# First attention and banded attention each in one written-out order, the neighbour sequences' projection, rotation and output between the heads; x loaded by sequence

## The chip, the cores and the metric

One NeuronCore of a Trainium2 chip runs one program. The metric is its device time in microseconds. Engines: TensorE (PE; its weight loads are PEld in the profile), VectorE (DVE), ScalarE (ACT), GpSimd (POOL) and SyncE (SP), which here only issues DMAs.

## The reference

Two layers of a decoder over x (4 sequences x 512 tokens x 512) in float32. Layer 0: an attention of 16 heads of 32 with 4 key/value heads and rotary positions, a residual and a layernorm; a mixing step with a context and experts of low rank; layer 1: an attention limited to a band, with biases, an RMS norm of queries and keys and rotary positions; a cross attention; rounds with a workspace. The two attentions are what the change touches:

```
q, k, v = x W_q, x W_k, x W_v           # layer 1: + biases; q, k normalised by their RMS per head
q, k = rope(q), rope(k)
p = softmax(q k^T * scale)              # layer 1: only keys j with 0 <= i - j <= 64
x = layernorm(x + (p v) W_o)            # layer 1: + bias
```

## The kernel before

The program is five stages, one function each, one after another: `rope_attention` (line 353, "stage 1"), `mixing_and_experts`, `window_attention` (line 1138, "the banded stage"), `cross_attention`, `workspace_rounds`. Every engine has an instruction order of its own, written out by Python loops; semaphores join them. PSUM has eight banks; `Banks` counts who filled and who freed each. `Core.start` (line 248) loads x, one DMA per sequence, and the identity, and ends in a wait for all five, before any stage begins.

Both attentions are staged alike and share the function `turns`, which gives the order of the parts on every engine:

```
heads(b); project(b + 1); output(b); keys(b + 1)      # b = 0, 1, 2; before them project(0), keys(0)
heads(3); output(3)
```

- **project**: PE transposes the 512 tokens of x in four blocks (line 598, stage 1; line 293, banded), ACT rounds each to float32r (line 302), DVE keeps the rest (line 309). Then for each tile t of 128 tokens, 24 products by three (lines 198 to 200, `split3`) of the halves of x and of W_q|W_k|W_v: 512 columns of queries into one bank, 256 of keys and values into the next. In stage 1 DVE reads them from PSUM: the cosine product (line 721), two sine products (line 732), and their sum (line 552). ACT copies values and four parts of the rotated queries and keys (lines 491 to 498), POOL subtracts the rounded parts (lines 462, 463) to fill the stacks `qs`, `ks`. In the banded stage DVE first adds biases (1379), takes mean squares (1384), ACT their square root (1303), DVE normalises (1394) and does the sine products (732), POOL the cosine product (721) and the stacks (1269, 1270), DVE the sum (1402).
- **keys**: PE transposes four key stacks (616; 1472), ACT copies them (508; 1330).
- **heads** of stage 1: a list `steps` of twenty rounds i, each of four steps t. In round i PE forms the four score tiles s of head i (634), whose maxima DVE takes (573), transposes the maxima of head i-1 (m, 642), forms the four transposed score tiles e of head i-2 (648), to which ACT applies the exponential (530), and transposes the queries of head i+1 (q, 627). Heads go in groups g of four. In rounds 4g+6 and 4g+7 PE multiplies the group's probabilities by values (o, 663) and by ones (666); POOL adds three of a head's four probability tiles first (472, 474) into `x_cur`, which has room for one group, so that from head 4 on its sums wait until the group before is full. In rounds 4g+8 and 4g+9 DVE divides (quotients d: 559, 561), and only then PE may start the next group. s has two banks, e three, q and m one, o two.
- **heads** of the banded stage: twenty-one rounds; per head one transpose of queries (1483) that DVE copies (1424), one block of scores with the mask (1490, 1494), one exponential (1340); every four rounds the attention products (1505, 1513) and quotients (1432, 1434).
- **output**: PE multiplies by W_o, four tiles (676; 1525); DVE adds x and takes statistics (327, 329, 338, 340), POOL raises to the power -0.5 (349), DVE normalises (344).

The weights are split by ACT (484; 1292) and POOL (454; 1254) before PE begins. The banded stage loads x anew into `x_cur` (284) and POOL adds the output bias to x (1261).

Of the kernel before, what the change touches and what calls it, by code (L numbers as in the profile page):

```python
# [202 lines left out]
class Core:  # L203


    def __init__(self, nc, ctx, d):
# [32 lines left out]
        self.s1_stacked, self.s4_stacked = primed("s1_stacked", T), primed("s4_stacked", T)  # L239
        self.s4_v_out, self.s4_roped = primed("s4_v_out", T), primed("s4_rope_parts", T)  # L240
# [4 lines left out]
        self.consts = sem("consts_loaded")  # L245
        self.pool_consts = sem("pool_consts_set")

    def start(self, stage):

        block = stage.enter_context(self.nc.Block())  # L250

        @block.sync
        def _(sp):
            for b in range(B):
                sp.dma_start(self.x[:, b * T:(b + 1) * T, :], self.d["x"][b].rearrange("(t p) d -> p t d", p=P)) \
                  .then_inc(self.consts, 16)
# [96 lines left out]
def rope_attention(c):  # L353

    nc, d, ps = c.nc, c.d, c.ps
    with ExitStack() as ctx:
        def sb(nm, shape, dt=F32):
            return ctx.enter_context(nc.sbuf_tensor(f"s1_{nm}", shape, dt))

        wq_hi = sb("wqkv_hi", [P, KD, NQKV], F32R)  # L360
        wq_lo = sb("wqkv_lo", [P, KD, NQKV], F32R)
        wo = sb("wo", [P, KD, D])
        qs = sb("q_stacks", [P, T, NH, STK])
# [5 lines left out]
        v = sb("v", [P, T, NK])  # L369
        v_next = sb("v_next", [P, T, NK])  # L370
        NPB = 6
        probsT = sb("probsT", [P, NPB, T, S])
        outT = sb("outT", [P, 4, S])
        inv = sb("inv_sums", [P, S])
        ra = sb("rope_a", [P, 2, NQK * HD])
        rb = sb("rope_b", [P, NQK * HD])
        cs = sb("cos_sin", [P, T, 2, HD])
        wraw = probsT[:, 0:3, :, :].rearrange("p a b c -> p (a b c)")[:, 0:KD * NQKV] \
            .rearrange("p (k n) -> p k n", k=KD)

        weights = c.sem("s1_weights_loaded")
        w_hi = c.sem("s1_w_hi_ready")
        w_lo = c.sem("s1_w_lo_ready")
        frame = c.sem("s1_constant_rows_set")
        roped = Count(c.sem("s1_roped"), T)
        v_out = Count(c.sem("s1_v_out"), 1)
        r_hi = Count(c.sem("s1_rope_hi"), T)
        stacked = c.s1_stacked
        added = Count(c.sem("s1_probs_added"), NH)

        steps = [("q", 0)]
        for i in range(NH + 4):
            g, r = (i - 6) // 4, (i - 6) % 4
            for t in range(T):
                if i < NH:  # L400
                    steps.append(("s", i, t))
                if 0 <= i - 2 < NH:
                    steps.append(("e", i - 2, t))
                if t == 0 and 0 <= i - 1 < NH:
                    steps.append(("m", i - 1))
                if t == 2 and i + 1 < NH:
                    steps.append(("q", i + 1))
                if 0 <= g < 4 and r < 2 and t % 2 == 0:
                    steps.append(("o", g, 2 * r + t // 2, 0))
                if 0 <= g < 4 and r == 1 and t % 2:  # L410
                    steps.append(("o", g, t // 2, 1))
                if 0 <= g < 4 and r >= 2 and t % 2:
                    steps.append(("d", g, 2 * (r - 2) + t // 2))

        steps = [s for s in steps if s[:2] != ("d", NKV - 1)]
        uses = []
        n = {"s": 0, "e": 0}
        for s in steps:
            if s[0] in "qm":
                uses.append((s, 5, 1))  # L420
            elif s[0] == "s":
                uses.append((s, n["s"] % 2, 1))
                n["s"] += 1
            elif s[0] == "e":
                uses.append((s, 2 + n["e"] % 3, 1))
                n["e"] += 1
            elif s[0] == "o" and s[2:] == (0, 0):
                uses.append((("o", s[1]), 6, 2))


        ps.open_segments({
            "heads": uses,
            "project": c.x_uses([2, 3]) + [(("p", t), (0, 3)[t % 2], 2) for t in range(T)],
            "output": c.y_uses([2, 5]),
            "keys": [(("k", g), (0, 1)[g % 2], 1) for g in range(NKV)]})

        block = ctx.enter_context(nc.Block())

        @block.sync
        def _(sp):  # L440
            sp.dma_start(wraw, d["l0a_wqkv"].rearrange("(k p) n -> p k n", p=P)).then_inc(weights, 16)
            sp.dma_start(cs[:, :, :, :], d["cos_sin"].rearrange("(t p) a n -> p t a n", p=P)).then_inc(weights, 16)
            sp.dma_start(wo[:, :, :], d["l0a_wo"].rearrange("(k p) n -> p k n", p=P)).then_inc(weights, 16)

        @block.gpsimd
        def _(pool):
# [4 lines left out]
            pool.memset(nmax[:, :, :, :], 0.0).then_inc(frame, 1)  # L451

            pool.wait_ge(w_hi, 1)
            pool.tensor_tensor(wq_lo[:, :, :], wraw, wq_hi[:, :, :].bitcast(F32), ALU.subtract).then_inc(w_lo, 1)

# [2112 lines left out]
```

## Time and profile before

| | us |
|---|---|
| median of 3 runs | 2774.46 (2773.37 to 2779.09) |
| the profiled execution | 2771.16, its span 2769.4 |
| PE busy | 2235.7 (81%) |
| DVE busy | 1512.0 (55%) |
| ACT busy | 1152.3 (42%) |
| POOL busy | 922.0 (33%) |

Times in the profile count from the span's start. PE's busy time has modelled ends of matmuls and is no measure of how well it is used. A line's "idle before, releaser" says what ended the engine's wait. A mean granted clock of 1.00 is TensorE's full clock.

### The profile page before, as it was taken

Reading aid. Unit: us, or ns where it says so; the run is one execution under the profiler, and the core shown is the slowest. Engines: PE = TensorE matmul, PEld = TensorE weight load, DVE = VectorE, ACT = ScalarE, POOL = GpSimd, SP = SyncE. Lnnn points to the kernel's source line nnn. Section 1 sums busy time; section 2 is a strip of 40 time slices with the busy share of each in tenths; the row PEclk is TensorE's granted clock in tenths of the full one; section 3 lists DMA queues with packets and bytes.
Section 4 is the critical chain, followed back from the end, with each engine's and each line's share of the span. In section 5 each row is a group of like instructions: output and inputs, shape, how many; then the busy total and the mean of one; then the engine's idle time right before and its main releaser. Section 6 shows DMA issues by size and latency. Waiting matters only on the chain. (4 is left out here: it accounts for less than half of the span.)

```text
span 2769.4 us, 34033 instructions
## 1 busy us (share of the span) xinstructions
PE 2235.7 (81%) x11600; PEld 1532.0 (55%) x11624; DVE 1512.0 (55%) x2234; ACT 1152.3 (42%) x2123; POOL 922.0 (33%) x553
## 2 busy tenths in 40 slices
PE   3888888857893668667699999999999999967672
PEld 3444545436672445444477777777777777743340
DVE  1656565634554475664255575557555755543435
ACT  2636363623422332322355555555555555531322
POOL 2424243420003120220355555555555555530101
PEclk9999999978996889888899999999999999988796
DMA  2000000010002000000311121112111111120001
GB/s 102 1 1 1 1 1 1 1 52 6 1 1 84 1 16 16 1 1 1 108 46 45 45 69 45 45 45 68 45 45 45 46 46 45 45 98 0 0 1 61
DMA packets 63213, 88.84 MB, mean 32 GB/s; under 512 B 6224, under 2 KB 41424, under 8 KB 62096
## 3 DMA queue, kind: packets, MB, share of 16 engines
q1 hardware_dynamic: 63120, 87.60, 9.4%
q8 instruction: 59, 0.97, 0.1%
q14 instruction: 34, 0.28, 0.0%
HBM read 75.00 MB, written 4.19 MB: 29 GB/s over the span
## 5 line engine op out<-in xcount | busy, mean ns | idle before, releaser
L1826 DVE RECIPROCAL s_inv_sums<-banks 128x512 f32<-128x512 f32 x64 | 214.8, 3356 | 343.2 <-PE banks L1939 339.8
L1700 POOL TENSOR_TENSOR s_qk_rstd<-s_mean_sq,minus_half 128x8 f32<-128x8 f32 x64 | 118.5, 1852 | 501.2 <-DVE s_mean_sq L1813 501.2
L573 DVE TENSOR_REDUCE s_neg_max<-banks 128x1 f32<-128x512 f32 x256 | 169.9, 687 | 117.6 <-PE banks L634 117.3
L1932 PE MATMUL banks<-s_probsT,s_v 128*128 128x512 f32 x512 | 230.8, 593 | 0.0
L1763 ACT ACTIVATE s_probsT<-banks,s_minus_bound,s_qk_rstd 128x512 f32<-128x512 f32 x256 | 177.0, 782 | 92.4 <-PE banks L200 88.4
L530 ACT ACTIVATE s_probsT<-banks 128x512 f32<-128x512 f32 x256 | 145.2, 599 | 107.8 <-PE banks L648 106.9
L198 PE MATMUL banks<-s_w_proj_hi,xT_hi 128*128 (+1 forms) x512 | 170.2, 332 | 2.9 <-DVE s_ctxT_lo L1874 2.9
L1932 PEld LDWEIGHTS banks<-s_probsT,s_v 128*128 128x128 f32 x512 | 97.5, 190 | 110.9 <-issue 108.2
L1734 ACT ACTIVATE s_squares<-banks 128x512 f32<-128x512 f32 x64 | 38.2, 597 | 286.6 <-PE banks L200 286.6
L1693 POOL TENSOR_TENSOR s_w_proj_lo<-s_w_proj_raw,s_w_proj_hi 128x2048 f32 (+1 forms) x33 | 152.0, 4607 | 12.7 <-ACT s_w_proj_hi L1726 12.7
L634 PE MATMUL banks<-s_kT,s_qT 96*128 96x512 f32 x256 | 123.1, 486 | 40.6 <-DVE s_neg_max L573 24.7
L1709 POOL TENSOR_TENSOR s_probs_pair_sums<-s_probsT 128x1024 f32<-128x1024 f32 x64 | 151.1, 2361 | 7.2 <-issue 7.2
L472 POOL TENSOR_TENSOR x_cur<-s_probsT 128x512 f32<-128x512 f32 x64 | 81.5, 1274 | 201.1 <-PE banks L666 139.4
L199 PE MATMUL banks<-s_w_proj_lo,xT_hi 128*128 (+1 forms) x512 | 145.3, 284 | 0.0
L200 PE MATMUL banks<-s_w_proj_hi,xT_lo 128*128 (+1 forms) x512 | 145.3, 284 | 0.0
L721 POOL TENSOR_TENSOR s_rope_a<-s_proj,s_cos_sin_gain 128x512 f32<-128x512 f32 (+1 forms) x32 | 29.9, 955 | 274.4 <-DVE s_proj L1394 274.4
L634 PEld LDWEIGHTS banks<-s_kT,s_qT 96*128 96x128 f32 x256 | 49.7, 195 | 125.2 <-issue 62.0
L1340 ACT ACTIVATE s_probsT<-banks,s_minus_bound 128x896 f32<-128x896 f32 x64 | 64.5, 1008 | 119.6 <-PE banks L1494 119.6
L198 PE MATMUL banks<-s_w_out_hi,s_outT_hi 128*128 (+1 forms) x256 | 104.2, 407 | 5.8 <-DVE s_outT_lo L1833 5.8
L198 PEld LDWEIGHTS banks<-s_w_proj_hi,xT_hi 128*128 128x128 f32 x512 | 98.4, 192 | 18.1 <-issue 18.1
L198 PE MATMUL banks<-s_w_proj_hi,s_ctxT_hi 128*128 (+1 forms) x256 | 101.5, 396 | 7.1 <-ACT s_v L1749 7.1
L199 PEld LDWEIGHTS banks<-s_w_proj_lo,xT_hi 128*128 128x128 f32 x512 | 98.5, 192 | 14.8 <-issue 14.8
(382 smaller groups left out, 6079.0 us busy)
## 6 DMA issues: line engine op xcount, KB each, us to landing
s_w_proj_raw<-l1x_wq SPq DMA_DIRECT2D x33, 512.0 KB, 4.7
s_w_out_raw<-l1x_wo SPq DMA_DIRECT2D x33, 512.0 KB, 3.9
s_w_proj_raw<-l1x_wk SPq DMA_DIRECT2D x33, 256.0 KB, 5.0
s_w_proj_raw<-l1x_wv SPq DMA_DIRECT2D x33, 256.0 KB, 5.1
x_cur<-x_all SPq DMA_DIRECT2D x8, 1024.0 KB, 6.9
x_all<-x SPq DMA_DIRECT2D x4, 1024.0 KB, 9.2
s_ctxT<-ctxT SPq DMA_DIRECT2D x8, 512.0 KB, 5.1
out<-x_all SPq DMA_DIRECT2D x4, 1024.0 KB, 4.3
```

What stands on the lines that cost most here:

```text
L198: pe.matmul(out, lhs[0], rhs[0], start=start, stop=False)
L199: pe.matmul(out, lhs[0], rhs[1], start=False, stop=False)
L200: return pe.matmul(out, lhs[1], rhs[0], start=False, stop=stop)
L530: act.activation(probsT[:, h % NPB, k, :], ps.ap(s), ACT.Exp).then_inc(ps.freed(s), 1)
L573: dve.tensor_reduce(nmax[:, h % 2, t, 0:1], ps.ap(s), AX.X, ALU.max, negate=True) \
L634: pe.matmul(ps.ap(s), qT[0:STK, h % NQB, t * P:(t + 1) * P], kT[0:STK, h % NKV, :], start=True, stop=True).then_inc(ps.filled(s), 1)
L1693: pool.tensor_tensor(out, raw, hi.bitcast(F32), ALU.subtract).then_inc(done.sem, 1)
L1700: pool.tensor_tensor(rs[:, j, :, :], ms[:, j, :, :], c.mhalf[:, 0:T * HP].rearrange("p (t h) -> p t h", h=HP), ALU.pow) \
L1709: pool.tensor_tensor(psum2[:, :, :], probsT[:, h, 0:2, :], probsT[:, h, 2:4, :], ALU.add)
L1763: act.activation(probsT[:, h, k, :], pb.ap(("e", h, k)), ACT.Exp, bias=bound[:, 0:1], scale=rs[:, 1, k, h:h + 1]).then_inc(pb.freed(("e", ...
L1826: dve.reciprocal(inv[:, h, :], pb.ap(("sum", h))).then_inc(pb.freed(("sum", h)), 1)
L1932: mm = pe.matmul(pb.ap(("o", h)), v[:, k, h * DX:(h + 1) * DX], probsT[:, h, k, :], start=(k == 0), stop=(k == T - 1))
```

## The change

Both functions drop `turns` and their parts. One list `seq` of steps (phase, sequence, ...) is built, and every engine walks the whole of it and does what of a step is its own. New phases: X (transpose of a block of x), Pq and Pk (a tile's query product; its key and value product), R (sine on DVE, cosine on POOL; in the banded stage normalisation before and the sum after), A (the sum, stage 1), H (ACT's copies and POOL's stacks), Y (a tile of the output product with its addition), L (normalisation), S (square roots of four tiles). In round i, step t, of sequence b in stage 1:

```
            extra = {(i, t): [] for i in range(LAST) for t in range(T)}
            if b > 0:
                for t in range(T):
                    extra[0, t].append(("d", b - 1, NKV - 1, t))
                    extra[t + 1, 1].append(("Y", b - 1, t))
                extra[5, 3].append(("L", b - 1))
            if b + 1 < B:
                for k in range(KD):
                    extra[4 + k // 2, 1 + k % 2 * 2].append(("X", b + 1, k))
                for t in range(T):
                    i = 7 + 2 * t if t < NPJ else 15
                    extra[i, 1].append(("Pq", b + 1, t))
                    extra[i + 1, 0].append(("Pk", b + 1, t))
                    extra[i + 1, 1].append(("R", b + 1, t))
                    extra[i + 1, 2].append(("A", b + 1, t))
                    extra[14 + t, 3].append(("H", b + 1, t))
```

and in the banded stage:

```
            if b > 0:
                for t in range(T):
                    extra[t].append(("Y", b - 1, t))
                extra[5].append(("L", b - 1))
            if b + 1 < B:
                for k in range(KD):
                    extra[2 + k].append(("X", b + 1, k))
                extra[14].append(("S", b + 1))
                for t in range(T):
                    extra[6 + 2 * t].append(("Pq", b + 1, t))
                    extra[7 + 2 * t].append(("Pk", b + 1, t))
                    extra[14 + t].append(("R", b + 1, t))
                    extra[15 + t].append(("H", b + 1, t))
```

The core of the rest, stage 1:

```diff
-            sp.dma_start(self.ident[:, :], self.d["ident"]).then_inc(self.consts, 16)
-            sp.wait_ge(self.consts, 16 * (B + 1))
...
+            sp.dma_start(c.ident[:, :], d["ident"]).then_inc(first, 16)
+            load_x(0, first)
+            sp.dma_start(w, d["l0a_wqkv"].rearrange("(k p) n -> p k n", p=P)).then_inc(weights, 16)
...
-            pool.tensor_tensor(wq_lo[:, :, :], wraw, wq_hi[:, :, :].bitcast(F32), ALU.subtract).then_inc(w_lo, 1)
+            pool.tensor_tensor(w_l[:, 0:2, :], w[:, 0:2, :], w_h[:, 0:2, :].bitcast(F32), ALU.subtract).then_inc(w_lo_pool, 1)
...
+                if ph == "R":
+                    t = s[0]
+                    pool.wait_ge(*sin_done.after(b, t + 1))
+                    rope_cos(pool, pj[:, t % NPJ, :], pj[:, t % NPJ, :], cs, t).then_inc(cos_done.sem, 1)
...
+                elif ph == "Pq":
+                    t = s[0]
+                    act.wait_ge(*ps.full(0, ("Pq", b, t)))
+                    if t >= NPJ:
+                        act.wait_ge(*stacked.after(b, t + 1 - NPJ))
+                    act.activation(pj[:, t % NPJ, 0:D], ps.ap(("Pq", b, t)), ACT.Copy).then_inc(ps.freed(("Pq", b, t)), 1)
...
+                elif ph == "L":
+                    act.wait_ge(*nmr_ready.after(b, 1))
+                    for t in range(T):
+                        xt = c.x[:, b * T + t, :]
+                        act.activation(xt, xt, ACT.Identity, bias=nmr[:, t:t + 1], scale=c.rstd[:, t:t + 1])
...
+                elif ph == "R":
+                    t = s[0]
+                    dve.wait_ge(*projected.after(b, t + 1))
+                    dve.drain()
+                    rope_sin(dve, pj[:, t % NPJ, :], rb, cs, t).then_inc(sin_done.sem, 1)
+                elif ph == "A":
+                    t = s[0]
+                    dve.wait_ge(*sin_done.after(b, t + 1))
+                    dve.wait_ge(*cos_done.after(b, t + 1))
+                    dve.tensor_tensor(pj[:, t % NPJ, :], pj[:, t % NPJ, :], rb[:, :], ALU.add).then_inc(roped.sem, 1)
```

NPJ is 3: the projected queries and keys go by ACT copies into three buffers in SBUF, where sine and cosine read them. DVE's step `d` of group 3 falls in round 0 of the next sequence. X, Pq, Pk and Y of the rounds use bank 4, which was the third bank of e; e keeps two. Values have two buffers instead of a copy. In the banded stage the same pieces use bank 3 (queries keep bank 2 alone); biases come into the products as one more product with a row of ones (four DMAs of single rows instead of two broadcast over 128 partitions); ACT instead of DVE reads the projection and copies queries; x is not loaded anew and POOL's addition to it goes; ACT waits for the weights alone before it splits them, POOL and DVE each take half of the low part; S takes the four tiles' roots at once.

## Rows read from the trace of the kernel before

**Rows 1.** Busy time by stretch (us, PE, PEld, DVE, ACT, POOL, PEclk, DMA, GB/s)
```profile
202.00:294.70 92.70, 79.72 (x444) 38.06 (x443) 57.31 (x92) 52.19 (x95) 40.41 (x32) 0.96 0.00 1
...
970.00:987.00 17.00, 16.99 (x97) 15.01 (x98) 14.10 (x24) 5.05 (x12) 1.89 (x2) 1.00 0.16 63
...
1081.00:1197.00 116.00, 81.02 (x579) 53.96 (x585) 72.45 (x109) 33.91 (x55) 20.08 (x18) 0.85 0.03 10
```

**Rows 2.** PE's timeline at the seams of stage 1 (start us, us, engine, line)
```profile
66.55 1.73 PE L616 MATMUL banks<-ident_sb,s_k_stacks 128*96 128x128 f32 x7 [6.23 <-POOL s_k_stacks L463]
...
294.73 1.09 PE L598 MATMUL banks<-ident_sb,x_all 128*128 128x128 f32 x8
...
316.61 13.90 PE L676 MATMUL banks<-s_wo,s_outT 128*128 128x512 f32 x32
330.35 1.04 PE L616 MATMUL banks<-ident_sb,s_k_stacks 128*96 128x128 f32 x8
```

**Rows 3.** PE's timeline, transposes of the maxima in five rounds
```profile
210.38 0.60 PE L642 MATMUL banks<-ident_sb,s_neg_max 128*32 128x128 f32 x4
...
214.07 0.60 PE L642 MATMUL banks<-ident_sb,s_neg_max 128*32 128x128 f32 x4
...
253.19 0.60 PE L642 MATMUL banks<-ident_sb,s_neg_max 128*32 128x128 f32 x4 [0.18 <-DVE s_neg_max L573]
...
260.72 0.60 PE L642 MATMUL banks<-ident_sb,s_neg_max 128*32 128x128 f32 x4
...
264.85 0.60 PE L642 MATMUL banks<-ident_sb,s_neg_max 128*32 128x128 f32 x4
```

**Rows 4.** Timeline of the end of a turn, POOL and PE
```profile
282.55 1.28 POOL L472 TENSOR_TENSOR x_cur<-s_probsT 128x512 f32<-128x512 f32 x1 [11.53 <-PE banks L666]
...
287.75 4.48 PE L663 MATMUL banks<-s_probsT,s_v 128*32 128x512 f32 x24 [1.06 <-DVE s_outT L561]
...
293.73 1.07 PE L666 MATMUL banks<-x_cur,ones_sb 128*32 128x512 f32 x8
```

**Rows 5.** Timeline of the start, ACT and POOL
```profile
25.46 2.76 ACT L484 ACTIVATE s_wqkv_hi<-s_probsT 128x3072 fp32r<-128x3072 f32 x1 [8.84 <-DMA s_wo<-l0a_wo]
28.30 6.65 POOL L454 TENSOR_TENSOR s_wqkv_lo<-s_probsT,s_wqkv_hi 128x3072 fp32r<-128x3072 f32 x1 [8.81 <-ACT s_wqkv_hi L484]
```

**Rows 6.** Groups of instructions by form, 0 to 600 us (busy, mean ns | idle)
```profile
L573 DVE TENSOR_REDUCE s_neg_max<-banks 128x1 f32<-128x512 f32 x256 | 169.9, 687 | 117.6 <-PE banks L634 117.3
...
L474 POOL TENSOR_TENSOR x_cur<-x_cur,s_probsT 128x512 f32<-128x512 f32 x64 | 81.7, 1276 | 9.1
...
L559 DVE RECIPROCAL s_inv_sums<-banks 128x128 f32<-128x128 f32 x64 | 60.7, 948 | 9.8 <-PE banks L666 9.7
...
L462 POOL TENSOR_TENSOR s_q_stacks<-s_rope_a,s_q_stacks 128x512 fp32r<-128x512 f32 x16 | 20.6, 1289 | 93.0 <-ACT s_k_stacks L498 93.0
L561 DVE TENSOR_TENSOR s_outT<-banks,s_inv_sums 128x128 f32<-128x128 f32 x64 | 18.7, 292 | 5.1 <-issue 0.4
...
L552 DVE TENSOR_TENSOR s_rope_a<-s_rope_a,s_rope_b 128x640 f32<-128x640 f32 x16 | 14.3, 892 | 1.2
L732 DVE TENSOR_TENSOR s_rope_b<-banks,s_cos_sin 128x320 f32<-128x320 f32 x32 | 14.1, 481 | 0.0
...
L495 ACT ACTIVATE s_q_stacks<-s_rope_a 128x512 fp32r<-128x512 f32 x16 | 10.0, 623 | 0.0
```

**Rows 7.** Timeline of one rotation of the banded stage, POOL and DVE
```profile
886.89 1.86 POOL L721 TENSOR_TENSOR s_rope_a<-s_proj,s_cos_sin_gain 128x512 f32<-128x512 f32 x2 [4.67 <-DVE s_proj L1394]
886.90 1.53 DVE L732 TENSOR_TENSOR s_mask_f<-s_proj,s_cos_sin_gain 128x256 f32<-128x256 f32 x1
```

**Rows 8.** Timeline of the banded stage: first product, first keys, last quotient's start
```profile
867.67 0.77 PE L198 MATMUL banks<-s_wqkv_hi,xT_hi 128*128 128x512 f32 x1 [1.61 <-DVE xT_lo L309]
...
910.16 3.71 PE L1472 MATMUL banks<-ident_sb,s_k_stacks 128*96 128x128 f32 x16 [23.62 <-POOL s_k_stacks L1270]
...
1306.36 0.96 DVE L1432 RECIPROCAL s_wqkv<-banks 128x128 f32<-128x128 f32 x1 [6.45 <-PE banks L1513]
```

More of the change, by code:

```diff
@@ L415, in rope_attention, with cnt @@
-        steps = [s for s in steps if s[:2] != ("d", NKV - 1)]
+        nmr = sb("ln_minus_mean_rstd", [P, T])
+        w = probsT[:, 0:3, :, :].rearrange("p a b c -> p (a b c)")[:, 0:KD * NQKV].rearrange("p (k n) -> p k n", k=KD)
+        def cnt(name, per=1):
+            return Count(c.sem("s1_" + name), per)
+        first, weights, table = c.sem("s1_first_x_loaded"), c.sem("s1_weights_loaded"), c.sem("s1_table_loaded")
+        wo_in = c.sem("s1_wo_loaded")
+        x_in = [None] + [c.sem(f"s1_x{b}_loaded") for b in range(1, B)]
@@ L671, in output, with turned @@
-            def output(b, pos):
-                pe.wait_ge(*ps.released(at("heads", pos[0]), ("o", NKV - 1)))
-                for t in range(T):
-                    ps.wait_empty(pe, pos, ("y", t))
+            pe.wait_ge(first, 32)
+            def turned(key, rows, source):
+                ps.wait_empty(pe, 0, key)
+                for t in range(T):
+                    mm = pe.transpose(ps.ap(key)[0:rows, t * P:(t + 1) * P], source(t), c.ident[:, :])
+                mm.then_inc(ps.filled(key), 1)
@@ L1287, in _, with turned_hi @@
-            turns(pool, project, nothing, nothing, output)
+                elif ph == "L":
+                    pool.wait_ge(*var_ready.after(b, 1))
+                    pool.tensor_tensor(c.rstd[:, :], c.veps[:, :], c.mhalf[:, 0:T], ALU.pow).then_inc(rstd_ready.sem, 1)
         @block.scalar
         def _(act):
-            act.wait_ge(weights, 16 * 9)
-            act.activation(w_h[:, :, :], w[:, :, :], ACT.Copy).then_inc(w_hi, 1)
+            def turned_hi(b, k):
+                act.wait_ge(*ps.full(0, ("X", b, k)))
+                act.activation(c.xhi[:, k, :], ps.ap(("X", b, k)), ACT.Copy).then_inc(x_hi.sem, 1)
@@ L1531, in window_attention, with projected @@
-        c.close(B)
+                    mm = pe.transpose(ps.ap(key)[0:rows, t * P:(t + 1) * P], source(t), c.ident[:, :])
+                mm.then_inc(ps.filled(key), 1)
+            def projected(key, b, t, lo, hi):
+                out = ps.ap(key)[:, 0:hi - lo]
+                ps.wait_empty(pe, 0, key)
+                for k in range(KD):
+                    split3(pe, out, (c.xhi[:, k, t * P:(t + 1) * P], c.xlo[:, k, t * P:(t + 1) * P]),
+                           (w_h[:, k, lo:hi], w_l[:, k, lo:hi]), k == 0, False)
+                if b == 0 and t == 0:
+                    pe.wait_ge(bias_lo, 1)
+                pe.matmul(out, ones[:, :], bias[:, lo:hi], start=False, stop=True).then_inc(ps.filled(key), 1)
```

1033 lines of the change are left out of this document (545 added, 488 removed).

## The prediction

> **What bounds the kernel now.** I read the busy table by stretch, then TensorE's (PE's) timeline at the seams between a sequence's parts, then one step of every round, then what GpSimd (POOL) and VectorE (DVE) wait for. Stage 1 runs from 0 to 588 us, the banded stage from 837 to 1333. While the sixteen heads of stage 1 run, no engine is full: PE 79.7 of 92.7 us, DVE 57.3, ACT 52.2, POOL 40.4; in a banded turn of 116.0 us PE has 81.0, DVE 72.5, POOL 20.1 [rows 1]. In stage 1 a turn is followed by a serial part: X and projection from 294.7 to 316.6 (21.9 us), output product to 330.35 (13.7 us), then keys [rows 2]. A round of the head loop, measured from one transpose of the maxima to the next, takes 3.7 us plain, 7.5 us with six attention products in it or before it, and 4.1 us where DVE has its first two quotients [rows 3]. So before the change the path is PE's order, with short waits for DVE; only at the end of a turn do POOL and DVE set it: POOL begins the sums of a group of heads at 282.55, having idled 11.5 us for the group before; PE's next attention product waits for DVE's quotients until 287.75, and its last, which needs POOL's sums, starts at 293.73 [rows 4].
>
> The profiled execution took 2771.2 us (span 2769.4 and 1.8 around it), the median shown is 2774.5, 3.3 above it. The sum goes against 2771.2.
>
> **Stage 1, start.** The four loads of x and their barrier go; weights are asked for at about 2 us and not about 15 (25.46 less the 8.84 of wait and the start of ACT's block). ACT had waited for weights, table and output weights, split at 25.46, POOL's low half took 6.65 us from 28.30, and only then PE could start, at 35 [rows 5]. After: about 2.6 MB must land first; from the old weight wait (as many bytes, some 10 us after issue) I take 11.5 us, ACT done at 14.3, POOL's half of the subtraction 3.3 us with DVE's beside it, projection starts near 17.6. But for sequence 0 the steps of a tile are now serial in ACT's order: copies 0.9, DVE's two sine products 0.7, POOL's cosine 1.6 (640 of width against 1.28 for 512), sum 0.9, four ACT copies 1.5 [rows 6], with hand-offs 6.1 us a tile, while PE needs 4.2 (17.0/4 [rows 1]). First projection done at 24; three more tiles 18.5, the first chain and POOL's end 7: keys at 49.4 instead of 66.5 [rows 2]. **-17**, and +2 because PE idles some 14 us before them: **-15**.
>
> **Stage 1, rotations between heads (three turns).** X and projection now lie in the rounds. PE's pieces are a query product of 2.75 us and a key product of 1.4 (17.0/4 in 2:1 of width [rows 1]). The crux is POOL's queue. Its sums for heads 4 and 5 stand ahead of R(0), and wait for group 0 of the attention, full only as round 7 ends; heads 8 and 9 ahead of R(2), heads 12 and 13, and H(0), H(1), ahead of R(3). Each sum is 2 x 1.28 plus a drain, 2.65 us [rows 6]. DVE waits in A for the cosine, and behind A stands its next maximum, without which PE can't transpose maxima. From the end of round 7: POOL sums to 5.6; DVE's sine reads SBUF and ends at 6.2; cosine to 7.9; A; maximum 0.7; transpose. What else each round gets is PE's piece or DVE's:
> - rounds 4, 5 (four X): +2.4; round 7 (query product): +2.8
> - round 8: 10.1 instead of 4.1, its key product inside that: +6.0; round 12 the same: +6.0
> - round 9: +1.2; round 10 (POOL free, but sine, cosine and sum in series on DVE): +3.0; round 11: +2.8; rounds 13 and 14: +0.5; round 15: +2.8
> - rounds 16 to 19: ACT's copy of tile 3 waits for H(0), which stands behind head 12's sums: ACT free at 4.7 after group 2 is full, POOL's row is then 12, H0, 13, H1, cosine 3 (end about 12.6), A to 14.5, three quotients of 1.24 (0.95 and 0.29 [rows 6]) to 18.3, then the last 24 products, 7 us: 25.4 against 12.3 (282.4 to 294.7): +13.1. POOL's stacks end at 23, inside that.
> Sum 40.6 for the 21.9 removed [rows 2]: +18.7 a turn, **+56**.
>
> **Two SBUF inputs.** In the banded stage a sine product of 256 columns took 1.53 us where POOL's cosine started 0.01 us before it [rows 7], and one of 320 columns took 0.48 in stage 1, where it reads PSUM [rows 6]. The change makes stage 1 read SBUF too, with POOL adding probabilities meanwhile. So I let A wait for one POOL add (1.1 us) in round 8, round 12 and the tail: 3.3 of the 40.6. Without it the whole sum is 10 us lower. The Trainium skill, "SBUF — State Buffer", section "Who interferes with whom", says that a DVE instruction with two SBUF inputs and a GpSimd instruction reading SBUF exclude each other for the whole instruction; by that rule the 3.3 stands, without it it would go; the trace agrees with the rule in those two rows.
>
> **Stage 1, output between heads (three turns).** Round 0 gets four quotients in front of maxima: +2.1; round 1 the first output block, waiting for them: +3.1; rounds 2 to 4 get 3.45 us each of PE less the 0.6 us that the plain round idles: +8.6. L: DVE waits at (5,3) for POOL's power, behind head 3's sums, then four ACT normalisations (2.4) stand before exponentials: +4.2, and +1.5 in two turns where X(3) follows. 18.0 for 13.7: **+13**, and **+3**. The end of the stage: one hand-off more, **+1**. Two score banks instead of three: 0; ACT's exponential had finished two products earlier in the plain rounds, and where ACT is held up PE is held by DVE too (if not, 1 us a round, in 9 rounds of three turns, +27).
>
> Stage 1: -15 + 56 + 13 + 3 + 1 = **+58**.
>
> **Banded stage.** Start: ACT splits when the weights land, not the last table, halves on two engines, X hidden: projection 17.5 us before 867.67; but the rotations of sequence 0 now all follow it: chain R0 4.4 + 3 x 6.6 + 3.8 = 28, where 23.6 us of waiting stood. Keys 8 us before 910.16 [rows 8]: **-8**. Each tile's 6.6 is POOL's cosine 1.9, sum 0.8, ACT's copies 1.8, POOL's stacks 1.75 and hand-offs: POOL does H(t-1) before the cosine of t [rows 6, 7]. Turns: PE's 81.0 [rows 1] less 8.5 for rounds 14 to 20 (estimate: two score blocks, one group and a quarter), plus 9 for keys, queries, X and output in one bank each, gives R(0) at 81 us; then the same chain of 28: 109 instead of 116. Rounds 14 to 20 hold only 12 us of other work, so that chain is bare. Without Y (turn 0) 92; without projection (turn 3) to the last group 70. 92 + 109 + 109 + 70 = 380 for 396.2 (910.16 to 1306.36 [rows 8]): -16, of which +3 for a PE that idles some 15 us in each tail (clock, below), the last normalisation +1: **-12**. The biases put into the products cost 1.4 and 0.9 us of PE a turn, inside the 109; what leaves DVE and POOL for it (bias additions) wasn't on the path after the keys. Queries and normalisation that ACT takes over from DVE cost nothing: ACT has 33.9 of 116 us [rows 1]; under that cover gone they would add 0.6 us a head. New bias loads stand on SP behind the weights and land before ACT has split those.
>
> In the banded turns PE's granted clock averaged 0.85 [rows 1], between its two levels (1.2 and 2.4 GHz), after waits in the rotations; longer ones come.
>
> Total +58 - 8 - 12 = **+38**: 2809 for the profiled execution, and 3.3 more for the median: **2812 us**.
>
> **Rivals.** (A, the forecast, 0.50.)
> (B, faster, 0.22) POOL doesn't decide: if sums of heads 4, 5, 8, 9, 12, 13 run before DVE needs the cosine (if ACT and PE lag enough behind, that is if R begins over 5.6 us after the group is full), rounds 8 and 12 cost 1.8 each and the tail 3. A turn falls by 20.4, three by 61: 2812 - 61 = 2751. For it: 13 us of PE idle in every head loop [rows 1]. Against: the 11.5 us wait of POOL for PE before its sums [rows 4] is in the order itself and stays.
> (C, slower still, 0.15) the two score banks bind: 2812 + 27 = 2839.
> (D, nearly level, 0.13) only the tails bind, rounds 8, 10 and 12 hide under PE's pieces: 4.2 + 4.2 + 2 a turn less, 2812 - 31 = 2781.
> That the change doesn't do what it says is excluded: the order is written out.
>
> **Numbers.** A measurement of this kernel tells 0.2% (5.5 us) from nothing. Faster: B and a few of A and D, 0.27; same: part of D, 0.06; slower 0.67. The range takes D, A, most of C and half of B: 2750 to 2842; A's own is 2790 to 2830.
>
> **What would show it.** Right: keys of sequence 0 near 49 us; turns of stage 1 near 155 us from key step to key step instead of 132; DVE's sum waiting for POOL's cosine about 2 us in rounds 8 and 12, 5 or more in round 16; ACT held at tile 3; in the banded stage about 28 us from the first rotation to the keys, PE mostly idle. Wrong: a stage 1 turn under 132 us, POOL's cosine never waited for, or PE busy over 90% of stage 1.

## The result and the profile after

The changed kernel took **2867.5 us** (median of 4 runs, 2866.5 to 2867.8); the kernel before, run beside it, 2776.8. The ratio is 1.0326, 95% interval 1.0311 to 1.0342. The direction was as forecast, the size was not: +91 us where +38 was forecast, and outside the range. The profiled execution has a span of 2864.6 us against 2769.4: 95.2 more, which is what the traces can be asked about.

Busy time of the changed kernel by stretch (stretch, its length, then PE, PEld, DVE, ACT, POOL with instruction counts, PEclk, DMA, GB/s). The first is the loop over heads of sequence 1, for 202.00:294.70 of [rows 1]; the second is a whole turn, keys to keys:

```profile
202.00:346.20 144.20, 111.22 (x518) 60.58 (x518) 73.66 (x117) 58.62 (x110) 41.57 (x33) 0.87 0.00 1
198.20:365.60 167.40, 127.65 (x612) 68.31 (x608) 79.92 (x126) 70.03 (x136) 55.12 (x45) 0.86 0.00 1
```

The same turn of the kernel before, in the same view:

```profile
198.10:330.30 132.20, 115.42 (x609) 62.90 (x608) 80.95 (x133) 64.59 (x125) 48.25 (x41) 0.97 0.00 1
```

And of run eleven below, which has its pieces between the heads as well:

```profile
176.80:307.90 131.10, 116.19 (x608) 63.97 (x608) 76.94 (x127) 69.92 (x136) 54.88 (x45) 0.93 0.00 1
```

A turn issues the same TensorE work in all three. Before, it filled 115.4 of 132.2 us, so at that clock 17 us a turn were all that any order could win. The change did not win them: in the turn shown TensorE idles 40 us, and its products take 12 us longer, at a granted clock of 0.86 for 0.97.

TensorE's timeline of the changed kernel (start, duration, engine, line, in brackets the idle time before and what ended it). The four key steps answer to 66.55 and 330.35 of [rows 2]; then transposes of the maxima, which mark the rounds as in [rows 3]: a round lasts from its transpose to the next. First those of rounds 8, 9 and 10 of turn 0, then of rounds 1 to 5 of turn 3:

```profile
53.85 3.71 PE L658 MATMUL banks<-ident_sb,s_k_stacks 128*96 128x128 f32 x16 [14.38 <-POOL s_k_stacks L500]
...
102.36 0.60 PE L658 MATMUL banks<-ident_sb,s_neg_max 128*32 128x128 f32 x4
112.55 1.01 PE L658 MATMUL banks<-ident_sb,s_neg_max 128*32 128x128 f32 x4 [2.95 <-issue]
120.53 0.60 PE L658 MATMUL banks<-ident_sb,s_neg_max 128*32 128x128 f32 x4
...
198.25 0.97 PE L658 MATMUL banks<-ident_sb,s_k_stacks 128*96 128x128 f32 x7
...
365.61 0.64 PE L658 MATMUL banks<-ident_sb,s_k_stacks 128*96 128x128 f32 x4
...
532.88 1.08 PE L658 MATMUL banks<-ident_sb,s_k_stacks 128*96 128x128 f32 x8
...
544.32 1.01 PE L658 MATMUL banks<-ident_sb,s_neg_max 128*32 128x128 f32 x4 [1.01 <-DVE s_neg_max L621]
554.35 0.60 PE L658 MATMUL banks<-ident_sb,s_neg_max 128*32 128x128 f32 x4
561.65 0.60 PE L658 MATMUL banks<-ident_sb,s_neg_max 128*32 128x128 f32 x4
568.94 0.60 PE L658 MATMUL banks<-ident_sb,s_neg_max 128*32 128x128 f32 x4
577.20 0.71 PE L658 MATMUL banks<-ident_sb,s_neg_max 128*32 128x128 f32 x4
```

The turns, key step to key step: 144.4, 167.4, 167.3, and 125.7 from the last keys to the last quotient (658.53). Before: 131.6, 132.2, 133.4 and 97.6. That is 109.9 longer in all, against keys of sequence 0 that stand 12.7 earlier. The last instruction before the banded stage ends 98.3 us later than before (935.5 for 837.2), and between it and the rotary stage nothing was changed. A plain round takes 3.6 us as before, a round with an output tile 7.3, the first of them 10.0. Rounds 7 and 8 take 10.3 and 10.2 us; bare, that is without any of the moved work, they take 7.5 and 4.1.

The banded stage of the changed kernel (key steps and last quotient, for [rows 8]):

```profile
1003.23 1.09 PE L1521 MATMUL banks<-ident_sb,s_k_stacks 128*96 128x128 f32 x4 [28.72 <-POOL s_k_stacks L1338]
1099.54 0.87 PE L1521 MATMUL banks<-ident_sb,s_k_stacks 128*96 128x128 f32 x3 [8.23 <-POOL s_k_stacks L1338]
1212.90 0.87 PE L1521 MATMUL banks<-ident_sb,s_k_stacks 128*96 128x128 f32 x3 [8.59 <-POOL s_k_stacks L1338]
1325.88 0.87 PE L1521 MATMUL banks<-ident_sb,s_k_stacks 128*96 128x128 f32 x3 [8.75 <-POOL s_k_stacks L1338]
...
1397.90 0.96 DVE L1491 RECIPROCAL s_rope_b<-banks 128x128 f32<-128x128 f32 x1 [6.39 <-PE banks L1584]
```

Counted from the last instruction of the stage before it (837.2 before, 935.5 after), the keys stand 5.2 us earlier; keys to last quotient take 394.7 us for 396.2, and what follows 3.5 longer. The stage gains 3.3 us, rounded parts apart, where 20 were forecast.

### The profile page after: what moved, and what is told of

Same layout as the page of the kernel before. It is cut to its first block and busy times, and to the rows that moved or that the text cites. A ratio compares the mean times of both kernels' runs of the same rounds, so it can differ in the third digit from the quotient of the medians.

```text
span 2864.6 us, 34181 instructions
## 1 busy us (share of the span) xinstructions
PE 2296.4 (80%) x11672; PEld 1557.4 (54%) x11672; DVE 1428.1 (50%) x2105; ACT 1230.8 (43%) x2281; POOL 931.2 (33%) x569
## 5 line engine op out<-in xcount | busy, mean ns | idle before, releaser
L511 POOL TENSOR_TENSOR x_cur<-s_probsT 128x512 f32<-128x512 f32 x64 | 81.3, 1270 | 365.4 <-ACT s_probsT L578 187.8
L701 PE MATMUL banks<-s_kT,s_qT 96*128 96x512 f32 x256 | 136.7, 537 | 55.9 <-DVE s_neg_max L621 50.1
L713 PE MATMUL banks<-s_qT,s_kT 128*128 128x512 f32 x256 | 112.4, 441 | 27.5 <-ACT s_probsT L578 26.4
L701 PEld LDWEIGHTS banks<-s_kT,s_qT 96*128 96x128 f32 x256 | 54.1, 213 | 137.3 <-issue 85.6
L198 PE MATMUL banks<-s_wqkv_hi,xT_hi 128*128 128x512 f32 (+1 forms) x256 | 95.7, 374 | 17.8 <-POOL s_wqkv_lo L1324 9.1
## 6 DMA issues: line engine op xcount, KB each, us to landing
x_all<-x SPq DMA_DIRECT2D x4, 1024.0 KB, 11.8
```

The source lines that it names most:

```text
L198: pe.matmul(out, lhs[0], rhs[0], start=start, stop=False)
L701: pe.matmul(ps.ap(key), qT[0:STK, h % NQB, t * P:(t + 1) * P], kT[0:STK, h % NKV, :], start=True, stop=True).then_inc(ps.filled(key), 1)
```

## The experiments

Fourteen kernels, each with 4 runs beside 7 runs of the kernel before on the same chip. They form four groups: one to four, five to eight, nine to twelve, thirteen and fourteen; the kernel before had medians of 2776.1, 2779.4, 2781.0 and 2776.3 us beside them. Ratios are to those. Microseconds "less" are against the kernel after, 2867.5 us, which was measured beside 2776.8; since the kernel before moved by up to 4.9 us from group to group, a difference of that size between two groups tells nothing.

**1. The banded stage taken back.** `window_attention` and its primed semaphores from the kernel before, all else from the kernel after.

> The banded stage of the kernel before put into the kernel after, so that only the rotary stage and the x loads are changed. Theory 1 (the two traces, stage by stage: the rotary stage lost about 98 us and the banded stage gave 3.3 back): 2867.5 + 3 = about 2871 us, 1.034 times the kernel before. Rival, my forecast for the banded stage (20 us gained, and hidden by something else in the trace): 2887 us, 1.040.

Measured: 2868.7 us, ratio 1.0335 (1.0318 to 1.0353), 1.2 over the kernel after. The 3.3 us that the trace gives the banded change lie inside this interval; the loss is the rotary stage's.

**2 to 4. Pieces back into blocks.**

```
-  extra[...].append(("X"...)), ("Pq"...), ("Pk"...), ("R"...), ("A"...), ("H"...)
+  behind the heads: seq += [("X", b + 1, k) ...]; per tile seq += [Pq, Pk, R, A, H]
```
```
-  extra[0, t].append(("d", b - 1, NKV - 1, t)); extra[t + 1, 1].append(("Y", b - 1, t))
+  before the keys: seq += [("d", b - 1, NKV - 1, t) ...] + [("Y", b - 1, t) ...]
```

> The kernel after, with x's transposes, projection and rotations of the next sequence in one block behind the heads again; the output product stays between the heads. Turn 0 of the changed rotary stage holds the projection pieces alone and took 144.4 us against about 96 for bare heads: 48.4 us for them. Theory 1 (the pieces cost three times 48.4 and a block costs about 23): 3 x 25 = 75 us less, 2792 us. Rival A (the heads themselves are slower, for their two banks of exponentials or the slower clock, and the pieces only show it): under 30 us less, 2840 us or more. Rival B (only the pieces' lockstep in the rounds, 18.7 a turn as I forecast, is given back): 56 us less, 2811 us.

> The kernel after, with the last group's quotients and the output product in one block ahead of the next keys; the normalisation on ScalarE stays in round 5, the rotations stay between the heads. Turn 3 of the changed rotary stage, with output product and normalisation alone, took 28 us over bare heads, about 5 of it the normalisation's round. Theory 1: 23 us between the heads against 13.7 in a block, three times 9 = 27 us less, 2840 us. Rival (as I forecast, 13.8 without the normalisation against 13.7): no change, 2867 us.

> The kernel after with both in blocks again (x's transposes, projection and rotations behind the heads, quotients and output product before the keys), but still with two banks for exponentials, ScalarE's copies and the start by sequence. Theory 1 (the places between the heads are the whole loss): 75 + 27 less, 2765 us, under the kernel before by the earlier start. Rival A (two banks of exponentials bind a round by 0.3 to 0.5 us, 64 heads): 2785 to 2800 us. Rival B (block and pieces are not additive, since each hides the other's waits): anything above 2800 us.

Measured: 2852.8 us, 1.0276 (1.0258 to 1.0293); 2871.9, 1.0344 (1.0327 to 1.0361); 2833.4, 1.0203 (1.0186 to 1.0220). My theory, that the place alone was the loss, fell in all three: 15 us less where 75 were expected, 4 more where 27 less were expected, 34 less where 102 were expected. Blocks in this form cost almost as much. The rounds of the fourth kernel say what did not cost: 3.6, 7.5, 4.1, as before, with two banks of exponentials. They also show a cost that has nothing to do with the blocks: round 6, behind the normalisation that stayed in round 5, takes 11.7 us where it takes 5.4 bare. What else cost stands in its VectorE timeline between turns 1 and 2:

```profile
327.14 1.65 DVE L760 TENSOR_TENSOR s_rope_b<-s_proj,s_cos_sin 128x320 f32<-128x320 f32 x2 [2.33 <-ACT s_proj L536]
...
333.69 1.61 DVE L760 TENSOR_TENSOR s_rope_b<-s_proj,s_cos_sin 128x320 f32<-128x320 f32 x2 [2.33 <-ACT s_proj L536]
...
344.40 0.96 DVE L621 RECIPROCAL s_rope_b<-banks 128x128 f32<-128x128 f32 x1
```

The same step of the kernel before, two tiles in a row:

```profile
308.45 0.82 DVE L721 TENSOR_TENSOR s_rope_a<-banks,s_cos_sin 128x640 f32<-128x640 f32 x1 [1.66 <-PE banks L200]
...
312.63 0.82 DVE L721 TENSOR_TENSOR s_rope_a<-banks,s_cos_sin 128x640 f32<-128x640 f32 x1 [1.61 <-PE banks L200]
```

In run four a tile goes ScalarE, VectorE, GpSimd, VectorE, ScalarE, and the next one's copies wait for the last: 6.5 us a tile (4.2 before, where VectorE reads PSUM). And my quotients stood behind all four tiles, so that the output block began only after TensorE had idled for 16.05 us. Bare heads are now known too: in run two, turn 0 has neither pieces nor output between its heads and takes 88.5 us from the keys to the last maxima; with 12.4 taken for the way from there to the last quotient (12.2 in turn 3 of the kernel before) that is 100.9. A later turn takes 97.6 (turn 3 of the kernel before).

**5. GpSimd's sums behind the cosine.** In GpSimd's order alone, the sums of heads 4 and 5, 8 and 9, 12 and 13 are put behind R(0), R(2), R(3).

> The kernel after, with one thing changed on GpSimd's queue alone: the sums of heads 4 and 5, 8 and 9, 12 and 13 stand behind the cosine step of tiles 0, 2 and 3 and no longer before it. Theory 1 (my forecast's crux: VectorE's sum waits for a cosine that waits for those sums; rounds 8 and 12 take 10.2 us each where bare ones take 4.1, round 15 15.7 where 6.9): about 4 us less in each of the three, 12 a turn, three turns: 36 us less, 2831 us. Rival (the tile's copies and the stack products are the lump, wherever the sums stand): under 10 us less, 2858 us or more.

Measured: 2843.0 us, 1.0234 (1.0204 to 1.0265), 24.5 less, where 36 were expected. Rounds 8 and 12 only fell from 10.2 to 9.6 us; round 15 fell from 15.7 to 9.6. The forecast had the sums in front of R(0) as what makes round 8 long. In the kernel after they had ended before VectorE was ready. The VectorE timeline of the kernel after in round 8:

```profile
105.26 0.95 DVE L628 RECIPROCAL s_rope_b<-banks 128x128 f32<-128x128 f32 x1
106.29 0.29 DVE L630 TENSOR_TENSOR s_outT<-banks,s_rope_b 128x128 f32<-128x128 f32 x1
106.65 1.49 DVE L767 TENSOR_TENSOR s_rope_b<-s_proj,s_cos_sin 128x320 f32<-128x320 f32 x2
108.06 0.68 DVE L621 TENSOR_REDUCE s_neg_max<-banks 128x1 f32<-128x512 f32 x1
109.87 1.80 DVE L612 TENSOR_TENSOR s_proj<-s_proj,s_rope_b 128x640 f32<-128x640 f32 x1 [1.12 <-POOL s_proj L756]
```

And GpSimd's:

```profile
106.13 1.26 POOL L513 TENSOR_TENSOR x_cur<-x_cur,s_probsT 128x512 f32<-128x512 f32 x1
108.22 1.54 POOL L756 TENSOR_TENSOR s_proj<-s_proj,s_cos_sin 128x640 f32<-128x640 f32 x1 [0.83 <-DVE s_rope_b L767]
109.72 1.26 POOL L511 TENSOR_TENSOR x_cur<-s_probsT 128x512 f32<-128x512 f32 x1
111.13 1.66 POOL L513 TENSOR_TENSOR x_cur<-x_cur,s_probsT 128x512 f32<-128x512 f32 x1
```

GpSimd waited 0.83 us for VectorE's sine, not the reverse. VectorE does in this one round four maxima, two quotients, a sine, a wait for the cosine and a sum.

**6 and 7. The output's side.** Six: VectorE's four last quotients ahead of the keys. Seven: also the adds of output tiles 0 to 2 behind the round's last maximum, and the normalisation's tiles in rounds 5 to 8.

> The kernel after, with VectorE's four quotients of the last group ahead of the next keys instead of between the first four maxima; nothing else. Theory 1 (the quotients stand before the maxima that the score products wait for, and the idle TensorE of round 0 then runs the first output block at the lower clock, 5.99 us for 3.59): 2.3 us of round 0 and about 2.4 of round 1 a turn, three turns: 14 us less, 2853 us. Rival (round 0 is held by the keys' copies anyway, the clock falls all the same): 0 to 5 us less.

> The kernel of the run before this one, with VectorE's add and statistics of three of the four output tiles behind the round's last maximum instead of before the next two, and with the normalisation spread over rounds 5 to 8, a tile in each. Theory 1 (TensorE waits 0.86 us in rounds 2 to 4 because 1.4 us of add and statistics stand before two maxima; the normalisation's 2.9 us on ScalarE stand before the exponentials and lengthen round 5 by 5.3): against the kernel after 14 for the quotients, 3 x 2.6 = 8 for the adds, 3 x 4 = 12 for the normalisation: 34 us less, 2833 us. Rival (TensorE is full in these rounds and nothing is to be had but the normalisation): 2850 us or more.

Measured: 2854.8 us, 1.0272 (1.0240 to 1.0304), 12.7 less; 2837.1, 1.0212 (1.0181 to 1.0243), 17.7 less again. In six the first maxima stand 8.1 us behind the keys instead of 11.4, yet round 1 still takes 9.9: the clock of that round is 0.71 and the output block in it 5.83 us long, 3.60 in the next. So the quotients' place cost 3.3 us a turn, but it was not what lowered the clock: the total came out as expected, half of the theory fell. In seven rounds 2 and 3 fell to 6.7, and the round behind the first normalised tile by 1.8 or more; the total, 30.4 less where 34 were expected, bears the theory out.

**8. The blocks done as before, on the new start.** Projection in bank pairs, rotation by VectorE from PSUM, quotients between x and projection, output product before the keys; normalisation in round 0.

> Start by sequence, split weights and the banded stage of the kernel after; the turns of the rotary stage as before: projection block behind the heads with the rotation read from PSUM by VectorE alone, quotients hidden behind it, output product before the keys; exponentials in two banks. The block run showed why it was slow: a tile took 6.5 us from sine to sine where the kernel before takes 4.2, and the quotients stood bare. Theory 1: turns of 132 us again, keys of sequence 0 some 13 us earlier, banded stage 3 less: 2776 - 16 = 2760 us. Rival (something else of the change costs in the blocks, the two banks or the copies): 2775 us or more.

Measured: 2754.2 us, 0.9916 (0.9886 to 0.9945). Theory 1 holds, a little under its 2760. Keys of sequence 0 stand at 46.3 us; turns of 138.1, 135.7 and 136.2, in a profiled execution that took 2762.1 us, 7.9 over the median.

**9. A tile's steps into rounds without quotients.**

```
-  extra[i + 1, 1].append(("R", b + 1, t)); extra[i + 1, 2].append(("A", b + 1, t))
+  j, k = ((10, 0), (11, 0), (14, 0), (16, 1))[t]
+  extra[j, k].append(("R", b + 1, t)); extra[j, (3, 3, 3, 2)[t]].append(("A", b + 1, t))
```

with the sums of heads 8, 9, 12 and 13 late in GpSimd's order.

> As in the run with the sums late, and the sine, cosine and sum of tiles 0, 1 and 2 moved to rounds 10, 11 and 14, which hold no quotients, with the sum on VectorE three steps behind the sine. In the run with the sums late rounds 8 and 12 still took 9.6 us each: VectorE had two quotients, the sine, a wait of 1.1 us for the cosine and a sum of 1.80 us (0.82 alone) in one round. Theory 1 (VectorE in its order is what these rounds wait for): rounds 8 and 12 fall to bare plus TensorE's own 1.4, about 5.5 us, rounds 10 and 14 grow by 1 to 2 each: 6 us less a turn, 18 in all, 2825 us. Rival (the pieces' TensorE work and its clock are the lump): under 5 us less, 2838 us or more.

Measured: 2801.4 us, 1.0081 (1.0058 to 1.0105): 66 us under the kernel after, 42 under run five, over twice what I expected of it. Rounds 8 and 12 take 5.5 us, as expected; I had expected rounds 10 and 14 to grow and they did not, and rounds 9 to 11 fell too (6.0, 7.2 and 10.3 for 7.5, 9.0 and 11.8).

**10. The output product in four pieces.** One product behind each score step, add and statistics behind the last maximum, quotients first.

> The kernel with the quotients first, and each output tile's four products one behind each score step of its round instead of all behind the second; add and statistics behind the round's last maximum; x's transposes a round later. In the block form a round took 7.3 us for 6.4 us of TensorE, which waited 0.88 for a maximum. Theory 1 (one block of 3.45 us leaves VectorE idle and then makes TensorE wait): rounds 2 to 4 fall to 6.6, round 1 by 1 to 1.5: 3.5 us less a turn, 10 in all, 2844 us. Rival (no gain, since TensorE alone fills the round and its clock decides): 2852 us or more.

Measured: 2833.2 us, 1.0192 (1.0168 to 1.0216), 21.6 under run six. TensorE's transposes of the maxima in its last turn:

```profile
524.95 1.05 PE L661 MATMUL banks<-ident_sb,s_neg_max 128*32 128x128 f32 x4
531.72 0.60 PE L661 MATMUL banks<-ident_sb,s_neg_max 128*32 128x128 f32 x4
538.07 0.60 PE L661 MATMUL banks<-ident_sb,s_neg_max 128*32 128x128 f32 x4
544.41 0.60 PE L661 MATMUL banks<-ident_sb,s_neg_max 128*32 128x128 f32 x4
```

A round with an output tile takes 6.35 us for 7.3, less than the 6.6 expected, and round 1 takes 6.8 for 9.9 (8.3 in turn 2), where 8.4 to 8.9 was expected: the run gained twice what I had expected of it.

**11 and 12. Everything mended, and the blocks with the normalisation late.**

> Everything that was found put together with the pieces still between the heads: quotients first, tile steps apart, sums late, output products split, the power on GpSimd ahead of the sum it stood behind, the normalisation's tiles in rounds 7 and 11, where ScalarE idles. Theory 1 (each wait adds its own): 2867.5 - 43 for sums and tile steps - 13 for the quotients - 10 for the split - 12 for the normalisation: 2790 us, still over the kernel before, because TensorE is full in the rounds and its 33 us of pieces a turn cost there what they cost in the blocks, plus the last tile's chain of 7 us behind the heads. Rival (TensorE has room in the heads, and with the waits gone the pieces are partly free): under 2765 us.

> The block version that came out at 2754 us, with the normalisation taken out of round 0: the power on GpSimd in round 0, the shift on VectorE in round 1, a tile each on ScalarE in rounds 7 and 11. In that version the first maxima stood 10.6 us behind the keys, 8.2 in the kernel before. Theory 1 (ScalarE's 2.9 us and VectorE's wait for the power stand before the first exponentials): 2.4 us a turn, three turns: 2747 us. Rival (the first scores wait for the keys' copies): no change, 2754 us.

Measured: 2754.8 us, 0.9907 (0.9881 to 0.9933), and 2755.6, 0.9916 (0.9893 to 0.9939). The mended pieces beat my 2790 by 35 and the kernel before by 0.9%. The 35 are what runs nine and ten had won beyond what I had put down for them, 23 and 12. The rival's number, under 2765, came true and its reason, that the pieces are partly free, did not, as the key steps of run eleven show:

```profile
53.95 1.30 PE L672 MATMUL banks<-ident_sb,s_k_stacks 128*96 128x128 f32 x5 [14.38 <-POOL s_k_stacks L514]
176.79 1.08 PE L672 MATMUL banks<-ident_sb,s_k_stacks 128*96 128x128 f32 x8 [0.58 <-POOL s_k_stacks L514]
307.93 1.08 PE L672 MATMUL banks<-ident_sb,s_k_stacks 128*96 128x128 f32 x8 [0.58 <-POOL s_k_stacks L514]
437.69 1.08 PE L672 MATMUL banks<-ident_sb,s_k_stacks 128*96 128x128 f32 x8 [0.58 <-POOL s_k_stacks L514]
```

Turns of 122.8, 131.1 and 129.8. Projection and rotation cost 21.9 us over bare heads in turn 0 (122.8 less 100.9), as much as they took as a block [rows 2]; output and normalisation cost 14.3 in turn 3 (549.62 for the last quotient, less 437.69 and 97.6), for 13.7. From the keys of sequence 0 to the last quotient run eleven takes 495.7 us, the kernel before 494.8: its gain comes from the start, where the keys stand 12.6 us earlier, and not from the turns. Twelve: the normalisation's place in round 0 had cost nothing that a median shows. Eleven and twelve have equal medians but not equal starts: twelve rotates sequence 0 from PSUM and has its keys at 45.8 us, eleven at 54.0; run fourteen takes that difference away.

**13 and 14. What was still open.** Thirteen is run nine with GpSimd's sums left in their old order; fourteen is run eleven with sequence 0 rotated from PSUM.

> The kernel after, with sine, cosine and sum of tiles 0, 1 and 2 in rounds 10, 11 and 14, and GpSimd's sums of probabilities left in their old order. With both changed the run was 66 us under the kernel after, with the sums alone 24.5. Theory 1 (VectorE's rounds with quotients and tile steps together are the larger part): 3 turns of (10.2 - 5.5) x 2 and the smaller rounds 10 and 11, about 14 a turn: 42 us less, 2825 us. Rival (tile steps help only where the sums no longer stand before them): under 20 us less, 2848 us or more.

> The version with the mended pieces between the heads, 2754.8 us, with the four tiles of sequence 0 rotated by VectorE straight from PSUM as in the block version, whose keys of sequence 0 stood at 46.3 us where the mended pieces have 54.0. Theory 1 (a tile through the copies, VectorE and GpSimd in turn takes 6.5 us, one read from PSUM 4.2): 7.5 us less, 2747 us. Rival (the start waits for the weights, not for the tiles): no change, 2755 us.

Measured: 2832.6 us, 1.0207 (1.0187 to 1.0226), 34.9 under the kernel after; and **2744.2 us**, 0.9883 (0.9864 to 0.9902), the fastest found. In thirteen rounds 8 and 9 are short (5.5 and 6.0 us), and GpSimd's queue shows itself one tile later: the sum of head 8 stands before the cosine of tile 1, VectorE's sum of that tile, the last step of round 11 in the order, waits for it, and round 12 takes 10.5 us where run nine has 5.5. Its VectorE timeline:

```profile
121.01 0.82 DVE L613 TENSOR_TENSOR s_proj<-s_proj,s_rope_b 128x640 f32<-128x640 f32 x1
...
135.46 1.80 DVE L613 TENSOR_TENSOR s_proj<-s_proj,s_rope_b 128x640 f32<-128x640 f32 x1 [4.99 <-POOL s_proj L757]
```

So both causes are there, 34.9 and 24.5 alone and 66.1 together. In fourteen the keys of sequence 0 start at 46.25 and turn 0 takes 120.3. Of the 27.3 us that its trace lies under that of the kernel before, 20.3 are the earlier keys and only 3.7 the turns (491.1 us from the keys of sequence 0 to the last quotient for 494.8). Against run twelve, the blocks on the same start, it needs 9.5 us less for the same stretch (491.1 for 500.6), with 11.4 between the medians; the two intervals of the ratios touch. Its key steps:

```profile
46.25 1.94 PE L691 MATMUL banks<-ident_sb,s_k_stacks 128*96 128x128 f32 x8 [6.47 <-POOL s_k_stacks L514]
...
166.51 1.08 PE L691 MATMUL banks<-ident_sb,s_k_stacks 128*96 128x128 f32 x8 [0.58 <-POOL s_k_stacks L514]
```

## Why the prediction missed

The forecast for the profiled execution was +38, it became +95.2. That is 57 too little, 40 of them in the rotary stage and 17 in the banded one.

**Start: the sign right, 5.6 too much.** Forecast -17 for the keys and +2 for a TensorE that idled before them; measured -12.7, and +3.3 for the heads of turn 0, whose first maxima stand 10.9 us behind the keys instead of 8.0 (the idle time was 14.38). The chain of a tile is 6.5 us where 6.1 was taken, and GpSimd's half of the split took 4.99 us, not 3.3. Run fourteen shows what the chain costs: 7.7 us at the keys and 2.6 in turn 0.

**Rotations between heads: the sum right, its mechanism half wrong.** 40.6 us a turn was forecast. Turn 0 took 43.5 over its bare heads. Round by round: 7 +2.8 (forecast 2.8), 8 +6.1 (6.0), 12 +6.1 (6.0), 15 and the tail together +16.1 (15.9), 9 to 11 +10.4 (7.0). But what made rounds 8 and 12 was VectorE's own order, two quotients and a tile's steps in one round, and hardly GpSimd's sums. With the sums late both rounds keep 9.6 of their 10.2 us (run five); with the tile steps elsewhere and the sums left alone round 8 falls to 5.5 (run thirteen). VectorE's sum waited 1.12 us for the cosine in round 8, where the forecast had about 2. So the right total came of a chain that began at the wrong engine. The sums do decide in round 15, by the path that the forecast named for tile 3, ScalarE's copy held until the stacks of tile 0 are made behind head 12's sum. ScalarE's timeline in round 15 of turn 1:

```profile
344.42 0.60 ACT L538 ACTIVATE s_proj<-banks 128x512 f32<-128x512 f32 x1 [10.73 <-POOL s_k_stacks L500]
```

With the sums late this wait is gone and round 15 takes 9.6 us for 15.7. The forecast had placed it behind the heads (+13.1, with +2.8 in round 15); measured are +8.9 in round 15 and +7.3 behind the last maxima. Those 7.3 stay in run five (19.5 us from there to the keys, bare 12.4), and no run separates what makes them. So rival B, that GpSimd's queue doesn't decide, was half true in its reason and wrong in its number. Its sum was wrong too: 4.2 in each of two rounds and 10.1 in the tail are 18.5 a turn, not 20.4. D and C fell (two score banks cost 0 in run four).

**Output between heads: the term that failed, +30 for three turns.** Forecast 18.0 a turn, measured 28.0 (125.7 less 97.6). By its steps: round 0 +2.3 (forecast 2.1); round 1 +5.9 (3.1), 2.4 of it because its block took 5.99 us for 3.59, at a granted clock of 0.70; rounds 2 to 5 +12.6 (8.6); normalisation +5.3 (4.2); the tail +1.8 (0). TensorE's timeline in rounds 1 and 2 of turn 3, the two blocks and a wait in the second:

```profile
545.56 5.99 PE L742 MATMUL banks<-s_wo,s_outT 128*128 128x512 f32 x8
...
555.25 3.59 PE L742 MATMUL banks<-s_wo,s_outT 128*128 128x512 f32 x8
...
561.10 0.47 PE L701 MATMUL banks<-s_kT,s_qT 96*128 96x512 f32 x1 [0.86 <-DVE s_neg_max L621]
```

The sentence that failed most is "3.45 us each of PE less the 0.6 us that the plain round idles", 4.0 of the 10 us a turn; the lower clock of round 1 had no term. I let the block use up TensorE's idle time, when it adds to it: while it runs VectorE has no new scores to work on, and after it 1.4 us of add and statistics stand before two maxima, for which TensorE waits 0.86. Runs seven and ten show it: with add and statistics behind the last maximum the round takes 6.7 us instead of 7.3, with the products spread over the round as well 6.35, and there the forecast's 2.9 a round would have held (2.7 over the plain 3.65).

**The sum.** Start 5.6, rotations of turn 0 2.9, turns 1 and 2 9.7 and 9.6 over their 157.7, turn 3 10.0 over its 115.6, end of the stage 0.1 (1.1 for 1): 37.9 of the 40. The rest is in the forecast's base: it took a turn of the kernel before as 97.6, 21.9 and 13.7 us, 399.6 for three, and they took 397.2.

**Banded stage: -20 forecast, -3.3 measured.** The chain was right, 27.8 us from the first rotation to the keys (1071.75 to 1099.54, forecast 28), and the same 27.8 in turns 1 and 2. TensorE's part before it was right too: the last product of the projection ends 64.2 us behind the keys in turn 0 and 81.3 in turn 1 (forecast 64 and 81). But the first rotation begins only at 68.5 and 85.6. A term was missing between the two. TensorE's last product of the projection of turn 0, and VectorE's timeline behind it:

```profile
1067.08 0.38 PE L1532 MATMUL banks<-s_bias_rows,s_ones_rows 33*128 33x256 f32 x1
1067.80 0.82 DVE L1465 TENSOR_REDUCE s_mean_sq<-s_squares 128x20 f32<-128x640 f32 x1 [6.68 <-ACT s_squares L1378]
...
1071.02 0.65 DVE L1471 RECIPROCAL s_qk_rstd<-s_rms 128x80 f32<-128x80 f32 x1 [2.14 <-ACT s_rms L1383]
1071.75 0.82 DVE L1477 TENSOR_TENSOR s_proj<-s_proj,s_qk_rstd 128x640 f32<-128x640 f32 x1
```

And ScalarE's at the same time:

```profile
1069.42 1.28 ACT L1383 ACT_TABLE_LOAD   x1
1070.72 0.27 ACT L1383 ACTIVATE s_rms<-s_mean_sq 128x80 f32<-128x80 f32 x1
1071.01 1.28 ACT L1411 ACT_TABLE_LOAD   x1
```

Mean square, table load, root and reciprocal stand between the last product and the first rotation: 4.3 us in each of the three turns, 12.9 of the 17, and the forecast has no line for them. This is read from the trace and no run changed it. At the start the keys came 5.2 earlier, not 8, and the end was 3.5 longer, not 1; the last turn took 72.0 us, not 70. So 2.8, 12.9, 2.0 and 2.5, less the 3 that the forecast had added for the clock in the turns, make up the 17.

**Two SBUF inputs.** In round 8 the sum of 0.82 us took 1.80 beside GpSimd's add of 1.26, and GpSimd's next add 1.66; the sine of two products took 1.49 for 0.90. Over the twelve tiles the sum's mean was 1556 ns, and 1061 in run nine, whose order keeps the adds away. By the Trainium skill, "SBUF — State Buffer", section "Who interferes with whom", a VectorE instruction with two SBUF inputs and a GpSimd instruction that reads SBUF exclude each other. The trace agrees: the sum of 1.80 us ends 0.7 us after the add beside it, about its own 0.82. The forecast's 3.3 us a turn for it was not tried by itself; the sums alone lost 2.0 us a turn against run nine (four times 1556 less 1061 ns).

## What to carry to other kernels

Work put between other work costs the bounding engine about its own time; here a turn's TensorE work was 115 of 132 us before the change, and all mended orders, in blocks or in pieces, came out at 130 to 138 us for a full turn. What they gained came for the most part from the start. So ask of such a change first how much idle time of the full engine it can reach, and then, for each slot, what every other engine already does in that round: a step that fits the mean load of VectorE (81 of 132 us) still costs 4.7 us in the one round in which the quotients stand (10.2 for 5.5, run thirteen). A piece of a bounding engine should be as small as the gaps between its hand-offs, and what follows from it on other engines should stand behind the step that the bounding engine waits for.

## What the runs showed that I had not expected

- The rotary stage's two exponential banks for three cost nothing: rounds of 3.6, 7.5 and 4.1 us in run four, as in [rows 3].
- Two effects of queue order add up to more than their sum: 34.9 and 24.5 us alone, 66.1 together, and 112.7 with the output's side mended too. Round 12 shows why: it falls to 5.5 us only when both are mended.
- The output block of round 1 stayed slow (5.83 us for 3.60) after the quotients had been taken out of round 0, at a granted clock of 0.71; with its four products spread the round fell to 6.8 (8.3 in one of three turns). What lowers the clock there stays open: in the 8.6 us before it TensorE had been busy for 5.8 and was still granted 0.94.
- The kernel in blocks (twelve) and the kernel in pieces (eleven) differ by 0.8 us in 2755, but the blocks have an 8.2 us better start. With the same start the pieces take 9.5 us less from the first keys to the last quotient (fourteen). Whether their place wins that, no run separates, since a tile's rotation goes another way in the two.
